# Arrival sums ahead of the first slot products on TensorE, and a signal of its own for GpSimd, in a graph attention layer on Trainium2

## The reference, cut to what matters

```python
h = relu(layernorm(x))                              # x: 8192 x 256
f1, f2 = h @ a[:256], h @ a[256:]
e = leaky_relu(f1 + f2.T, 0.2)
U = softmax(where(adj > 0, e, -9e15), axis=1)       # adj: 8192 x 8192 of 0 and 1
prop = U @ h;  rowsum = sum(U * 0.5 * U, axis=1)
feat = coe[2] * (prop - h*rowsum) + (1 - coe[2]) * (h + prop - h*rowsum)
feat = shrink(feat, 1e-6)
pu = U @ feat
out = x + mix(feat, pu, rowsum, coe, h0)            # elementwise
```

## Time and profile before

| | us |
|---|---|
| median of 3 runs | 1396.14 |
| lowest and highest of them | 1393.45, 1404.81 |
| the profiled execution | 1397.94 |
| its span, from the first instruction to the last | 1396.3 |

### The profile page before, as it was taken

One profiled execution on the slowest core, in us unless ns is written; L12 is line 12 of the kernel. 1 busy time (PEld: TensorE's weight loads), 2 busy tenths in 40 slices (PEclk: granted clock), 3 DMA queues, 4 the chain that ended last, 5 costly groups with the idle time before them and its releaser, 6 DMA issues.

```text
span 1396.3 us, 27742 instructions
## 1 busy us (share of the span) xinstructions
PE 921.4 (66%) x3629; PEld 565.3 (40%) x3630; DVE 932.3 (67%) x5233; ACT 861.6 (62%) x1840; POOL 589.4 (42%) x649
## 2 busy tenths in 40 slices
PE   3555666777766666767767777777656556676665
PEld 2431244444444433333333334334335444454443
DVE  7766656657888888888888888888782222334454
ACT  4675476778888888888888888888524221211111
POOL 2014335434433233232222222212377777777775
PEclk9985687879999999999888887877757877888999
DMA  6988887879999999999999999999236655777886
GB/s 173 353 323 323 294 344 279 314 281 383 372 384 364 377 381 379 385 378 390 387 382 368 381 382 372 370 377 374 66 95 186 183 170 172 220 227 224 253 255 202
DMA packets 152837, 423.14 MB, mean 303 GB/s; under 512 B 31111, under 2 KB 114697, under 8 KB 136406
## 3 DMA queue, kind: packets, MB, share of 16 engines
q1 hardware_dynamic: 122492, 345.66, 66.5%
q0 software_dynamic: 30304, 77.05, 18.0%
HBM read 398.37 MB, written 33.90 MB: 310 GB/s over the span
## 4 chain that ended last, share of the span: by engine, by line
DVE 27%; issue 24%; PE 16%; DMA 13%; POOL 6%; ACT 6%; DVEq 3%; ACTq 3%; POOLq 2%; SPq 0%
PE ACC L689 6%; DMA W<-feat_d,IDT 4%; DMA pt_d<-R 4%; POOL W L634 4%; PE TP L321 3%; DVE XHO L1053 2%; PE MISC L974 2%; ACT SG L309 2%; DMA R<-sc_d 2%; DMA R<-in_x_dram 2%; POOLq L623 1%; PE ACC L693 1%; POOL R L634 1%; DVE RE L1185 1%; ACTq L682 1%
## 5 line engine op out<-in xcount | busy, mean ns | idle before, releaser
L309 ACT ACTIVATE SG<-W,ABOVE 128x4096 bf16<-128x4096 f32 x126 | 467.0, 3706 | 60.9 <-DVE cnt L1036 50.9
L634 POOL DMA_INDIRECT R<-haug_d,IDS x230 | 230.3, 1002 | 585.7 <-issue 572.8
L321 PE MATMUL TP<-SG,FOLD 128*128 128x512 bf16 x1008 | 292.3, 430 | 0.0
L680 ACT ACTIVATE DG<-ident,WSR 128x128 f32<-128x128 f32 x230 | 75.7, 391 | 268.5 <-PE ACC L694 253.0
L1739 DVE SCALAR_TENSOR_TENSOR R<-ACC,SELF,R 128x256 f32<-128x256 f32 x63 | 30.5, 484 | 214.1 <-PE ACC L694 214.0
L688 PE MATMUL ACC<-XHO,ZB 128*128 128x256 bf16 x126 | 39.5, 313 | 190.7 <-DMA W<-feat_d,IDT 92.2
L689 PE MATMUL ACC<-R,DG 128*128 128x256 f32 x446 | 156.6, 501 | 0.0
L321 PEld LDWEIGHTS TP<-SG,FOLD 128*128 128x128 bf16 x1008 | 111.4, 119 | 110.0 <-issue 46.4
L634 POOL DMA_INDIRECT W<-feat_d,IDR x140 | 134.3, 959 | 42.7 <-issue 39.6
L689 PEld LDWEIGHTS ACC<-R,DG 128*128 128x128 f32 x446 | 102.6, 246 | 17.8
L688 PEld LDWEIGHTS ACC<-XHO,ZB 128*128 128x128 bf16 x126 | 12.4, 98 | 222.4 <-DMA W<-feat_d,IDT 113.0
(11 more groups left out here) (295 smaller groups left out, 2258.2 us busy)
## 6 DMA issues: line engine op xcount, KB each, us to landing
W<-in_adj_dram SPq DMA_DIRECT2D x128, 2048.0 KB, 10.0
haug_d<-R POOLq DMA_DIRECT2D x8, 1056.0 KB, 9.7
HTS<-haug_d SPq DMA_DIRECT2D x64, 132.0 KB, 9.7
R<-in_x_dram SPq DMA_DIRECT2D x8, 1024.0 KB, 6.6
R<-in_x_dram SPq DMA_DIRECT2D x64, 128.0 KB
R<-in_L_gnn_h_dram SPq DMA_DIRECT2D x64, 128.0 KB
R<-feat_d SPq DMA_DIRECT2D x64, 128.0 KB
out_dram<-R SPq DMA_DIRECT2D x64, 128.0 KB, 1.8
```

The costliest lines, as they stand in the source:

```text
L309: nc.scalar.activation(SG[:, u, half(h)], W2[:, u, half(h)], ACT.Sign, scale=2.0 ** 100, bias=ABOVE[:], accum_out=DEG[:, u, h:h + 1]).then ...
L321: nc.tensor.matmul(KP[u], FOLD[:, b], SG[:, u, b * FW:(b + 1) * FW], start=False, stop=False)
L634: pool.indirect_dma_start(out=g[:, k, 0:w], out_offset=None, in_=table, in_offset=bass.IndirectOffsetOnAxis(ap=ids[:, k:k + 1], axis=0), * ...
L680: nc.scalar.mul(DG[:, u, k], ident[:], weights[:, k:k + 1])
```

## The change

TensorE's arrival sums of tile t now stand ahead of the first products of tile t-2, not behind them. Since `ctl_ready` then no longer tells that these products are through, TensorE drains after them and gives a new signal, `firsts_ready`, for which GpSimd waits beside `ctl_ready`. In turns 0 and 1 there are no such products, and the signal starts at 2.

```diff
@@ first_gpsimd, body
                 pool.wait_ge(ctl_ready, t + 1)
+                pool.wait_ge(firsts_ready, t + 1)
                 gather_slots(pool, t + 1, G[:, u], IDS[:, u], haug_d, AUG, gathered[u], lambda: others_free(t),
                              bounds_check=N - 1, oob_is_err=False)
@@ first_tensor, body
                     nc.tensor.matmul(SPW, RE[:, ub], WS[:, ub, 0:K], start=True, stop=True).then_inc(w_spread, 1)
-                    slots = slots_of(pe, tb + 1)
-                    pe.wait_ge(diag_begun, tb + 1)
-                    first_products(pe, slots, ub, G[:, ub])
                 if live(0):
                     pe.wait_ge(counts_ready, t + 1)
                     nc.tensor.matmul(SUMS[:, 0:KC], ONESB[:], RC[:], start=True, stop=True)
                     nc.tensor.matmul(SUMS[:, KC:2 * KC], TRI[:], RC[:], start=True, stop=True).then_inc(sums_made, 1)
+                if live(2):
+                    slots = slots_of(pe, tb + 1)
+                    pe.wait_ge(diag_begun, tb + 1)
+                    first_products(pe, slots, ub, G[:, ub])
+                    pe.drain().then_inc(firsts_ready, 1)
+                if live(0):
                     if live(-2):
                         fold(pe, t + 2, q + 1, u, 0, NB // 4)
                     pe.wait_ge(edges_ready, t + 1)
@@ first_tensor, ahead of the first turn
             pe.sem_inc(prod_ready, 2)
+            pe.sem_inc(firsts_ready, 2)
```

More of the change, by code:

```diff
@@ L578, in adj_preln_kernel @@
         others_begun = sem("others_begun")
+        firsts_ready = sem("firsts_ready")
         gathered = [sem(f"gathered{u}") for u in range(2)]
```

## The result

The changed kernel takes 1556.58 us (median of 4 runs, 1555.92 to 1560.52) beside 1398.48 us for the kernel before: a ratio of 1.114, with a 95% interval of 1.111 to 1.117. It is slower by 158 us, where 120 were forecast; the time lies just above the range, whose upper end was 1555. (The prediction's chances speak of a forecast band of 1480 to 1560, in which 1556.6 lies; its stated range ended 5 us lower.)

What follows compares the result with a forecast made beforehand. VectorE's chain was taken to set the turn. 50 turns at +2.3 us give 115, other turns 7.1, so +122 us on 1397.9: 1520, adjusted to 1518 and then 1516 us; range 1455 to 1555.

Steps and rivals of the forecast that it cites:

- Which clock: TensorE's lower clock falls on products and fold in many turns; middle of full and half clock taken, +2.3 us a turn.
- RC to the products (sums' start, load): On TensorE, sums start 0.06 us after RC, then the slot count's register load takes 0.65 us.
- products and drain: TensorE's opening and 2.76 products, 1.31 us at full clock or 2.6 at half, then the drain, 0.3 or 0.6.
- fold's quarter: TensorE's stretch from L317 to where SPR can start: 1.07 us at full clock, 2.1 at half.
- SPR to L1191: From SPR on TensorE to VectorE's line that waits for it: 0.44 us at full clock, 0.6 at half.
- the clock falls in every turn: Rival: TensorE's path at half clock in every turn, +3.7 us each, +195 us in all, 1591 us; chance 0.07.
- The load: TensorE's slot count load behind the sums, with nothing queued to cover it: between free and 0.65 us, 0.65 taken.
- The drain: TensorE's drain after the first products: between 0.1 and 0.6 us, 0.3 taken; the skill's page made it 0.1 to 0.2.
- GpSimd: Its second wait, ahead of the gathers, costs nothing in turns 10 to 59; 0.5 us each in turns 61 and 62.
- Turns 2 to 9: Turns 2 to 7 make up the delay in waits for a store, 0, at most +8; turns 8 and 9 +4.6 together.

Runs made afterwards that it cites:

- load and clock together: Changed kernel with the slot count's load ahead of the wait for VectorE's counts and 24 matmuls on zeros behind SPW: ratio 1.026 to the kernel before.

## Why the prediction was right or wrong

**The sign, the place and the way: right.** It said that SPR would be late in every turn because the products go from a hole to the path from RC to L1191, and that VectorE would wait there with nothing to do. The wait for SPR was to pass 100 us and took 176.8; the sums' wait was to fall to 0.15 us a turn and fell to that; the idle piece ahead of the sums was put at 4 us and is 3.9. The runs bear it out: taking the load, the fold or the half clock off this path takes part of the loss back each, and load and clock together three quarters of it (1.026 for 1.114).

**The size: wrong, by the step "Which clock".** The sum was made at full clock (3.8 us from RC to L1191) and at half (6.6), and the middle taken, "+2.3 us a turn". The turn grew by 3.01, and the path from RC to L1191 by 3.09. By the prediction's terms, at the middle and as measured in turns 10 to 59:

| term, us a turn | middle | measured |
|---|---|---|
| RC to the products (sums' start, load) | 0.71 | 0.82 |
| products and drain | 2.4 | 2.95 |
| fold's quarter | 1.6 | 1.80 |
| SPR to L1191 | 0.5 | 0.41 |
| sum | 5.2 | 5.98 |

The term that carries the miss is "products and drain": 0.55 us of the 0.8. The products were at half clock not in half of the turns but in all 50: by the starts of L689 and L317 the stretch takes 2.3 us with two slots, 3.1 to 3.2 with three and 4.0 with four, where two slots take 1.36 at full clock. Only the fold's quarter was mixed (half clock throughout in 21 turns, full in 3), and SPR was at full clock again in 30. So the rival "the clock falls in every turn", which got 0.07, was right about the products and wrong about the rest. The argument against it, that the dense matmuls bring the higher level back, holds only from the fold on: in these turns the half clock lay on what stood right behind the idle piece, and that was the path. What was there to be read: in the trace before, an idle piece of 1.4 to 1.9 us stands ahead of the sums in 16 turns, and the fold behind it begins at half clock in 11 of them, that of the earlier trace rows among them, and at full in 5. That made half clock behind a piece twice as long the likelier price for the products; that it would be all 50 turns no row before showed. The Trainium skill's rule that rest means the low clock (TensorE: Matmul & The Clock Gate, What's actually happening) leaned that way; the trace after agrees with it, in all 50 turns behind 3.7 to 4.2 us of idle time.

**The load: right, 0.65 us taken, 0.69 measured** when it was moved away, and worth 44 us of the 158; 0.69 us a turn are the load itself, and the 0.2 that the turn gained besides lie in the products and the fold, which ran a little faster behind it. Without this term the forecast would have been some 35 us lower.

**The drain: right in size, 0.3 taken, 0.38 measured** at full clock; at half 0.6 was taken and 0.4 measured. The Trainium skill's rule against it (TensorE: Matmul & The Clock Gate, The mechanism), that the last matmul's signal is enough, was not put to use as it stands: the number of products changes from tile to tile, and the extra matmul that was added to carry the signal took as long (1556.0 against 1556.6 us). No run here shows what a signal on a matmul that runs anyway would give.

**GpSimd: right.** It sat 12.43 us before its first gather in the turn shown. For turns 60 to 62, with GpSimd's part, 2.5 us were forecast. Turns 60 and 61 alone cost 3.0; turn 62 can't be told apart from what follows it.

**Turns 2 to 9: 0 and +4.6 forecast, +0.8 measured for all eight.** Turns 2 to 7 absorb the delay, as said. Turn 8 is 4.3 us shorter and turn 9 3.7 longer: in turn 8 ScalarE still waits for the store of tile 0, 6.6 us before and 1.0 now, so this store covered one more turn than I took.

**One meeting place too few.** The rivals treated SPR as the only place at which TensorE meets VectorE. The kernel with the products behind SPR shows that MOV is a second one, close behind.

## What to carry to other kernels

In a loop like this, work that fills a hole between two waits is free only there; moved behind the second wait it lies on the chain with everything that it drags along, its register load and its drain too. When a move makes two short idle pieces of TensorE into one long one, price the work right behind it at half clock (here it was so in all 50 turns behind 3.9 us) and look whether that work is on the path. A signal that comes earlier by 0.2 us is worth 0.2 us a turn at most, and the way to the next one has to be summed before it is bought.

## What the runs showed of the hardware that had not been expected

- Reading a count from memory into a register on TensorE cost 0.7 us where nothing was queued on the array: "issue" idle of 0.53 us before L689 in the turn shown, though the load itself is 0.31.
- Twenty-four matmuls that compute nothing, 2.8 us of them a turn, made the changed kernel 71 us faster. In the kernel before, 8 of them were worth 0.3%.
- The same program took longer on other chips. On three of four the kernel before took 1531 to 1543 us, not 1398. Its first pass was nearly the same there, 13.45 us a turn against 13.23, and its second was not: from turn 62 to the end of the span 493 us against 382. Waits of GpSimd in the second pass, on the first chip and then on one of the others:

```profile
POOL W L634 <- issue: 39.6, 130, 0.3
```

```profile
POOL W L634 <- issue: 112.7, 140, 6.9
```

Between these gathers GpSimd pauses 0.3 us on the first chip and never longer, on the other now and then for up to 6.9. It is not GpSimd alone: of the steps of the sequencers that only compute, move or compare registers and wait for no signal, 2516 in the second pass of the kernel before, none takes over 0.5 us on the first chip, and on the other 247 do, on every engine but VectorE. What holds them was not tried. Each chip was used for one group of runs only, so chip and moment can't be told apart either. The changed kernel itself was run on the first chip alone.
